# Second expert loop: the down step as plain fp32 products of unsplit operands; the last layer's gate ratio in a buffer of its own

## What is computed

```python
logits = xt @ router_w.T + routing_bias
topk_p, topk_idx = jax.lax.top_k(jax.nn.sigmoid(logits), 2)
...
g = jnp.einsum('th,eih->tei', xt, wg)      # 256 -> 512
u = jnp.einsum('th,eih->tei', xt, wu)
h = jax.nn.silu(g) * u
y = jnp.einsum('tei,ehi->teh', h, wd)      # 512 -> 256
routed = jnp.einsum('te,teh->th', w, y)
```

```python
h = jax.nn.relu(base[:, :, None, :] + lora)
expert_out = jnp.einsum('bsef,df->bsed', h, Wo)
out = jnp.einsum('bse,bsed->bsd', w, expert_out)
```

## Time and profile before

| | us |
|---|---|
| median of 3 runs | 1835.18 |
| the runs' range | 1834.2 to 1836.62 |
| profiled execution, its own time | 1835.47 |
| its span, first to last instruction | 1833.7 |
| PE busy | 1463.2 (80%) |
| DVE busy | 1183.3 (65%) |
| ACT busy | 895.6 (49%) |
| POOL busy | 751.0 (41%) |
| second expert loop, PE work | about 1079 to 1311 |
| last layer, unit products | 1696.7 to the end |

### The profile page before, as it was taken

The page is one execution under the profiler, slowest core; times in us unless marked ns, Lnnn a source line. Parts: engine busy times, 40 slices in busy tenths (PEclk is TensorE's granted clock), DMA queues, the critical chain, the costliest instruction groups (busy, mean ns, idle before and its releaser), DMA issues. The chain is left out here.

```text
span 1833.7 us, 31460 instructions
## 1 busy us (share of the span) xinstructions
PE 1463.2 (80%) x10097; PEld 1281.1 (70%) x10114; DVE 1183.3 (65%) x2584; ACT 895.6 (49%) x1915; POOL 751.0 (41%) x797
## 2 busy tenths in 40 slices
PE   1699983799999999579996679999676935463898
PEld 0457773799999999346786679989675822243787
DVE  6356645588878887257656658888472447777444
ACT  4244441677777777135542346666324416454242
POOL 2222201466666666203212138778401930135244
PEclk8899985899999999799987789999898977785699
DMA  4000002556565563310002126666320010001001
GB/s 162 1 1 1 1 10 83 219 209 235 187 239 200 219 229 131 93 39 1 1 1 81 70 87 203 209 200 209 101 70 27 1 50 0 1 29 54 1 12 35
DMA packets 60158, 169.74 MB, mean 93 GB/s; under 512 B 11728, under 2 KB 40912, under 8 KB 50848
## 3 DMA queue, kind: packets, MB, share of 16 engines
q1 hardware_dynamic: 51232, 144.40, 22.8%
q0 software_dynamic: 8832, 24.13, 4.2%
HBM read 150.16 MB, written 18.35 MB: 92 GB/s over the span
## 5 line engine op out<-in xcount | busy, mean ns | idle before, releaser
L1468 POOL TENSOR_TENSOR l0m_e_DL<-l0m_e_DN,l0m_e_DH 128x256 fp32r<-128x256 f32 x184 | 185.4, 1015 | 119.1 <-ACT l0m_e_DH L1321 74.1
L1268 PE MATMUL PS<-l0m_e_CH,l0m_e_UH 128*128 128x256 f32 x736 | 210.9, 287 | 1.5 <-DVE l0m_e_CL L1398 1.5
L1268 PE MATMUL PS<-l0m_e_CH,l0m_e_UL 128*128 128x256 f32 x736 | 209.2, 284 | 0.0
L1268 PE MATMUL PS<-l0m_e_CL,l0m_e_UH 128*128 128x256 f32 x736 | 209.1, 284 | 0.0
L1370 DVE TENSOR_TENSOR l0m_e_UL<-l0m_e_U,l0m_e_UH 128x512 fp32r<-128x512 f32 x184 | 146.7, 798 | 5.7 <-ACT l0m_e_UH L1312 5.6
L1268 PEld LDWEIGHTS PS<-l0m_e_CH,l0m_e_UH 128*128 128x128 f32 x736 | 142.2, 193 | 1.9 <-ACT l0m_e_UH L1312 1.9
L1268 PEld LDWEIGHTS PS<-l0m_e_CL,l0m_e_UH 128*128 128x128 f32 x736 | 142.1, 193 | 0.0
L1268 PEld LDWEIGHTS PS<-l0m_e_CH,l0m_e_UL 128*128 128x128 f32 x736 | 141.9, 193 | 0.0
L1382 DVE SCALAR_TENSOR_TENSOR l0m_e_HR<-PS,l0m_e_BU,l0m_e_SG 128x256 f32<-128x256 f32 x184 | 88.8, 483 | 75.2 <-ACT l0m_e_SG L1329 72.4
L1329 ACT ACTIVATE l0m_e_SG<-PS,l0m_e_BU 128x256 f32<-128x256 f32 x184 | 87.5, 475 | 85.7 <-PE PS L1268 73.6
L1312 ACT CAST l0m_e_UH<-l0m_e_U 128x512 fp32r<-128x512 f32 x184 | 112.8, 614 | 13.9 <-DMA l0m_e_BU<-in_l_b 13.9
(11 more groups left out here) (515 smaller groups left out, 4695.5 us busy)
## 6 DMA issues: line engine op xcount, KB each, us to landing
l0m_e_U<-in_l_up SPq DMA_DIRECT2D x23, 2048.0 KB
l0m_e_DN<-in_l_down SPq DMA_DIRECT2D x23, 1024.0 KB
l1m_e_U<-in_l_up SPq DMA_DIRECT2D x23, 1024.0 KB
l1m_e_DN<-in_l_down SPq DMA_DIRECT2D x23, 512.0 KB, 3.9
l0m_c_GA<-results_by_choice SPq DMA_DIRECT2D x16, 256.0 KB, 3.7
l1m_c_GA<-results_by_choice SPq DMA_DIRECT2D x16, 256.0 KB, 3.0
l0m_e_BD<-in_l_b_rows SPq DMA_DIRECT2D x23, 128.0 KB
X<-in_x SPq DMA_DIRECT2D x4, 512.0 KB, 5.9
```

Source lines behind the costliest of these rows:

```text
L1268: ins = nc.tensor.matmul(hb(f)[:, a * SLOTS:(a + 1) * SLOTS], w[:, f % RING, k, a, :], x[:, j, k, :], start=(p == 0), stop=(p == len(passe ...
L1468: nc.gpsimd.tensor_tensor(DL[:, f % RING, :], DN[:, j, f, :], DH[:, f % RING, :].bitcast(F32), ALU.subtract).then_inc(s_dl, 1)
```

## The change

In `expert_tiles` a flag `split` is true for the first loop, whose program stays as it is, and false for the second. There DH, DL, HR, HH and HL are gone. DVE's product of the hidden chunk goes straight into HF, held for two tiles, in fp32. `down` is one plain fp32 product per 128 rows, of HF with the loaded DN, so 2 in place of 6 per chunk. ACT loses `down_high` and `hidden_high`, DVE loses `hidden_low`, POOL loses `down_low` and gets two writes of two elements (TICK) per tile. DN(t) now waits for `s_y`, the down products of tile t-2, in place of `s_dl`. In `l3_ffn` WB gets a buffer of its own, the copy no longer waits for WOL, and `first` waits for the two LT pieces; unit 2, which writes the PSUM bank of the third piece, waits for its copy.

```diff
@@ expert_tiles @@
+            split = weights.bias is not None
...
-                HR = sb_in(c, f"{tag}_HR", [P, RING, SLOTS])
-                HH = sb_in(c, f"{tag}_HH", [P, 2, NF, SLOTS], F32R)
-                HL = sb_in(c, f"{tag}_HL", [P, 2, NF, SLOTS], F32R)
+                if split:
+                    HR = sb_in(c, f"{tag}_HR", [P, RING, SLOTS])
+                    HH = sb_in(c, f"{tag}_HH", [P, 2, NF, SLOTS], F32R)
+                    HL = sb_in(c, f"{tag}_HL", [P, 2, NF, SLOTS], F32R)
+                else:
+                    HF = sb_in(c, f"{tag}_HF", [P, 2, NF, SLOTS])
...
+                TICK = sb_in(c, f"{tag}_TICK", [P, 4])
@@ sync: load(i, j) @@
                             if begun(i, j, 2):
-                                sp.wait_ge(s_dl, count(i, j - 1, 0))
+                                sp.wait_ge(s_dl if split else s_y, count(i, j - 1, 0))
                                 weights.down(sp, e, j)
@@ tensor: down(i, j, f) @@
+                            else:
+                                pe.wait_ge(s_hr, n + 1)
+                                if f == 0:
+                                    pe.wait_ge(s_down[j % 2], 16 * (i + j // 2 + 1))
                             if f == 0 and begun(i, j, 2):
                                 pe.wait_ge(s_ycopy, 2 * i + j - 1)
+                            if not split:
+                                for r in range(R):
+                                    ins = nc.tensor.matmul(yb(j)[:, r * D:(r + 1) * D],
+                                                           HF[:, j % 2, f, r * P:(r + 1) * P], DN[:, j % 2, f, :],
+                                                           start=(f == 0 and r == 0), stop=(f == NF - 1 and r == R - 1),
+                                                           skip_group_check=True)
+                                ins.then_inc(s_y, 1)
+                                return
@@ scalar: tile(i, j) @@
-                                if chunk_begun(i, j, f, NF - 2):
+                                if split and chunk_begun(i, j, f, NF - 2):
                                     down_high(i, j - 1, f + 2)
-                                if chunk_begun(i, j, f, 1):
+                                if split and chunk_begun(i, j, f, 1):
                                     hidden_high(i, j, f - 1)
@@ vector: hidden(i, j, f) @@
+                            if not split and begun(i, j, 2):
+                                dve.wait_ge(s_y, count(i, j - 2, f) + 1)
...
-                                ins = nc.vector.tensor_tensor(HR[:, f % RING, :], second, SG[:, f % RING, :], ALU.mult)
+                                ins = nc.vector.tensor_tensor(HR[:, f % RING, :] if split else HF[:, j % 2, f, :], second,
+                                                              SG[:, f % RING, :], ALU.mult)
@@ gpsimd: tile(i, j) @@
+                                elif f in (1, PUT):
+                                    n = 2 * t + (f == PUT)
+                                    if begun(i, j, 1) or f == PUT:
+                                        pool.wait_ge(s_dl, n)
+                                    nc.gpsimd.tensor_tensor(TICK[:, 0:2], IDENT[:, 0:2], IDENT[:, 0:2],
+                                                            ALU.subtract).then_inc(s_dl, 1)
@@ l3_ffn @@
-                WB = WO.rearrange("p n d -> p (n d)")
+                WB = sb_in(c, "l3f_WB", [P, T])
...
-                                pe.wait_ge(s_cp, 3 * (n + 1))
+                                pe.wait_ge(s_cp, 3 * n + 2)
+                            if u == 2:
+                                pe.wait_ge(s_cp, 3)
...
                             else:
-                                if n == 0:
-                                    act.wait_ge(s_wl, 2)
                                 nc.scalar.copy(WB[:, cols], PS[:, piece_bank(q), :]).then_inc(s_cp, 1)
```

More of the change, by code:

```diff
@@ L1275, in down @@
                             n = count(i, j, f)
-                            pe.wait_ge(s_dh, n + 1)
-                            pe.wait_ge(s_dl, n + 1)
-                            pe.wait_ge(s_hh, n + 1)
-                            pe.wait_ge(s_hl, n + 1)
+                            if split:
+                                pe.wait_ge(s_dh, n + 1)
+                                pe.wait_ge(s_dl, n + 1)
+                                pe.wait_ge(s_hh, n + 1)
+                                pe.wait_ge(s_hl, n + 1)
+                            else:
+                                pe.wait_ge(s_hr, n + 1)
+                                if f == 0:
+                                    pe.wait_ge(s_down[j % 2], 16 * (i + j // 2 + 1))
                             if f == 0 and begun(i, j, 2):
                                 pe.wait_ge(s_ycopy, 2 * i + j - 1)
+                            if not split:
[6 more added lines that the diff above has]
+                                return
                             for r in range(R):
@@ L1356, in _ @@
                         turns(act, tile)
-                        hidden_high(*LAST, NF - 1)
-                        for f in range(2, NF):
-                            down_high(*LAST, f)
+                        if split:
+                            hidden_high(*LAST, NF - 1)
+                            for f in range(2, NF):
+                                down_high(*LAST, f)
                     @block.vector
@@ L1377, in hidden @@
                             dve.wait_ge(s_silu, n + 1)
-                            if chunk_begun(i, j, f, RING):
+                            if split and chunk_begun(i, j, f, RING):
                                 dve.wait_ge(s_hl, n - RING + 1)
+                            if not split and begun(i, j, 2):
+                                dve.wait_ge(s_y, count(i, j - 2, f) + 1)
                             second = hb(f)[:, SLOTS:2 * SLOTS]
@@ L1430, in _ @@
                         turns(dve, tile)
-                        hidden_low(*LAST, NF - 1)
+                        if split:
+                            hidden_low(*LAST, NF - 1)
                         out_rows(*BEFORE_LAST)
```

13 lines of the change are left out of this document (8 added, 5 removed).

## The result

The changed kernel has a median of 1843.77 us over 20 runs, against 1835.66 us over 20 runs of the kernel before on the same chip: ratio 1.0048, 95% interval 1.0031 to 1.0065. It is slower by 0.5%; the forecast was 1824 us. The profiled execution took 1843.97 us, its span is 1842.2 (before 1833.7).

What follows compares the result with a forecast made beforehand. The second expert loop was taken as bound by a chain from down load to next tile's first product. Loop -7.3, its end -0.4 and last layer -3.7 sum to -11.4 against 1835.5: 1824 us, range 1816 to 1836.

Steps and rivals of the forecast that it cites:

- Step 1: Second expert loop: plain down products add 0.15 us a chunk, 0.60 a tile, making PE's own tile 9.43 us.
- the change of kind: Rival: switching between plain and fp32r products costs up to 0.08 us at 8 changes a tile, total 1832 us; 8%.
- four passes: Rival: a plain product costs four passes at the fp32r price, tile 9.79 us, total 1829 us; 4%.
- Step 2: ACT, DVE and POOL lose split work; this counts for nothing except 0.61 us less in C.
- C: Time from ACT's copy of the up weights to PE's first product of the tile: 3.2 us, forecast 2.6.
- Step 3: The down load, and the up load behind it on SP, now go out at tile's end, 2.4 us later.
- Step 4: Puts no longer start with the down load, so X shrinks from 8.9 to 7.5 us, bounds 6.8 and 8.9.
- X: Time from the down load's issue to ACT's copy of the up weights behind it: mean 8.9 us, forecast 7.5.
- the later DN decides: Rival: the down load goes out 2.4 us later and X does not shrink, total 1837 to 1850 us; 21%.
- Step 5: Two periods (2p) are one tile's work plus X and C: 19.53 us, 9.77 a tile, loop -7.3 us.
- Step 6: At the second expert loop's end, five chunks cost +0.75 and a 1.20 us wait goes: together -0.4 us.
- Step 7: Last layer: PE's 3.66 us wait goes, -3.7 us; -1.8 if the clock's rise stays at its hour.

Runs made afterwards that it cites:

- e4: Kernel before, split products kept, with SP issuing the next tile's up weights before the down load in the second expert loop: 1831.97 us, ratio 0.9981.
- e7: Kernel before, split products kept, with up weights first in the second loop and the gate ratio in its own buffer: 1820.83 us, ratio 0.9915.
- e3: Changed kernel with SP issuing the next tile's up weights before waiting to issue this tile's down weights: 1808.69 us, ratio 0.9853.
- e8: Kernel before, split products kept, with the down load also waiting for the down products of tile t-2: 1859.41 us, ratio 1.0137.
- e12: Changed kernel with two scratch subtractions on POOL ahead of each gather of the second loop, puts not shifted: 1840.50 us, ratio 1.0034.
- e13: Changed kernel with four scratch subtractions on POOL ahead of each gather of the second loop, puts not shifted: 1835.73 us, ratio 1.0007.
- e11: Changed kernel with three extra 128x128 products on PE ahead of each tile's wait for its up weights: 1835.79 us, ratio 1.0012.
- e1: Kernel before with only the last layer's change, the gate ratio in its own buffer: 1824.86 us, ratio 0.9930.
- e5: Kernel before with four plain products filling PE's 3.7 us wait in the last layer, the wait kept: 1827.87 us, ratio 0.9968.
- e2: Changed kernel with the last layer's part undone, leaving only the plain products and their new wait: 1857.63 us, ratio 1.0109.

## Why the prediction was wrong, step by step

**What bounds the kernel now: failed.** The chain from the down load to the next tile (8.9 + 3.2) explained the period to 0.4 us, and I took that for proof. It was not the only bound: with the loads out of the way (e4, e7) the split tile still takes 10.0 to 10.2 us. Its bound goes with the splits (e3 against e7), and the trace of e4 puts it on DVE. PE's own tile was also misread: the 8.83 us between the first two turns hold one chunk of tile 0, which has no down products. The next distance is 9.07.

**Step 1, the products: right.** A chunk takes 2.30 us (0.86 for two plain products), and no hole at the change of kind appears in e3's ten tiles at 96.4 of 96.4 us busy. The tile is 9.63 and not 9.43, by the misreading above. The rivals on the change of kind and on four passes are ruled out by it.

**Step 2, the other engines: right in C (2.5), wrong as "counts for nothing".** The removed splits are the very thing that the change gains, 0.4 to 0.5 us a tile; it shows only when the loads are mended (e3 against e7).

**Step 3, the wait: right, and the cause.** The step called it the loss in the change. e8 has it alone and loses 24.6 us; e3 takes it off the up load's path and the changed kernel becomes the fastest of all.

**Step 4, X: failed, the largest term.** I subtracted the puts and took 7.5; it was 9.3. In the sum that is 1.8 / 2 x 18 = 16 us of the loop. Nothing shows that the puts' departure shortened X: in the changed kernel most puts start 6 us or more behind the down load, and X grew. And I had written that the gather now "falls on the start of DN" and priced it at nothing: by e12 and e13 it may be worth 0.5 to 0.7, about as much as X's mean differs between executions. What else lengthened X stays open. An X that does not shrink is the rival "the later DN decides", which had 21%: with X = 9.3 its sum gives 2p = 9.43 + 9.3 + 2.6 = 21.3, a loop of 28.3 + 18 x 10.67 = 220.3, +8.9, in all 1840.

**Step 5, the period: lacked a term.** With the measured sizes 2p = 9.63 + 9.3 + 2.5 = 21.4, 10.7 a tile, which the evenly stalled pairs (21.5) and e11 (10.79) show. The changed kernel has 11.31. The other 0.6 us a tile are 13 us in the loop. About 10 of them are the clock, which fell six times behind stalls of 2.3 us and more; the rest is not taken apart. No step spoke of the clock in this loop, though step 7 did for the other layer.

**Step 6, the loop's end:** too small to be told apart in the ledger.

**Step 7, the last layer: the hole right, the clock's part missed.** -10.7 for -3.7; the hole is 3.4 of it (e1 against e5), the clock the rest. I asked whether the rise of the clock would stay at its hour, and so lose half; counted from the first gate product it came 20 us earlier instead (23 us for 43), once PE no longer paused (e5, e1).

The sum by measured terms: +24.4 loop, -10.7 last layer; the ledger's rest is run to run.

## What to carry to other kernels

A load that waits for a buffer also holds everything behind it in its queue: before a change that makes a wait later, look at what is issued behind it, and put the load that is needed first in front. A period explained by one chain is not proved until that chain is taken away; two bounds can lie within 0.1 us of each other, and then the gain of a change shows only together with another one. On TensorE a stall can cost more than its length, here 1.7 us more each time the granted clock fell behind it. So look at the clock in the windows behind each stall, and not at the stalls alone: filling them can pay even where the wait itself stays.

## What the runs showed of the hardware

- Behind a stall of 2.45 us PE's granted clock fell from 1.00 to 0.50 some 1.3 us into the work that followed, and stayed there for 3.4 us; six such falls stand in the changed kernel's loop, none in that of e11, where three extra products in each stall left 1.4 us as the longest. The stall's length alone does not decide it: behind one of 2.43 us in the same loop the clock stayed at 1.00, and in e12 it fell behind one of 1.76.

```profile
1143.10 0.38 PE L1276 MATMUL PS<-l1m_e_CH,l1m_e_UH 128*128 128x256 f32 x1 [1.76 <-ACT l1m_e_UH L1333]
...
1144.50:1147.90 3.40, 3.40 (x15) 3.04 (x14) 1.11 (x2) 0.89 (x2) 0.73 (x1) 0.50 0.86 282
```

- In the kernel before, after the hole of 3.66 us, the last layer's products ran at 0.50 for another 19.2 us, PE busy for 18.5 of them; with the hole filled (e5) or removed (e1) the clock rose 23 us after the first gate product in place of 43. With the hole kept the hour is not fixed either: in e2 the clock rose to 1.00 for 3.4 us 13 us after that product, and for longer at 34. The Trainium skill ("TensorE: Matmul & The Clock Gate", Part 1) says that the gate follows how busy PE has been. The effect of filling a hole agrees with it; that a nearly full PE stayed at 0.50 for 19 us does not follow from it, and no run here explains that.
- A pair of loads of 1.5 MB took 9.3 us (the changed kernel's mean X) with a gather of 0.25 MB beginning at its start, and 8.8 and 8.6 us with it 1 and 3 us later (e12, e13). That is about as much as this mean differs between executions of one loop (8.3 to 8.9), so it is a hint and not a finding.
